# An attention and mixture-of-experts block on one core: the rotary base chain moved forward, routing's side work on GpSimd and ScalarE, the last sums divided

## The reference, cut to what matters

```python
x  = input                                   # (8, 512, 128)
xn = layernorm(x)                            # xs1 in the kernel
# branch 1: attention with one shared query/key base
xn2 = layernorm(xn) * ln_w + ln_b            # xs2 in the kernel
uv = silu(xn2 @ uv_w.T + uv_b)               # 256 u, 256 v, 128 base
base = rope(base * gamma + beta)             # two of them: q and k
kern = square(relu(q @ k.T / sqrt(128) + bias[j - i]))
attn = (u * (kern @ v)) @ o_w.T + o_b + xn
# branch 2: shared MLP and the 2 of 8 experts with the largest sigmoid(xn @ W_router)
w  = topk_probs / (sum(topk_probs) + 1e-6)
ffn = sq_relu(xn @ W_sh_up) @ W_sh_down + sum over the 2 experts of w * sq_relu(xn @ W_up[e]) @ W_down[e]
return x + attn + ffn
```

## Time and profile before

| What | us |
|---|---|
| median of three runs | 392.57 |
| lowest and highest of them | 390.35, 453.52 |
| the profiled execution | 391.36 |
| its span, first to last record | 389.5 |
| TensorE busy / VectorE / ScalarE / GpSimd | 351.0 / 275.1 / 228.4 / 171.0 |

### The profile page before, as it was taken

How to read it: one execution, slowest core, us unless ns; L and a number is a source line. 1 busy time by engine, 2 the same in 40 slices (tenths; PEclk the granted TensorE clock), 3 DMA queues, 4 the chain that set the end, 5 groups by cost and what they waited for, 6 DMA issues and landing times.

```text
span 389.5 us, 6982 instructions
## 1 busy us (share of the span) xinstructions
PE 351.0 (90%) x1984; PEld 269.4 (69%) x1985; DVE 275.1 (71%) x646; ACT 228.4 (59%) x418; POOL 171.0 (44%) x161
## 2 busy tenths in 40 slices
PE   1779979989989999999996999999999999999791
PEld 1565658556556565756644989899899999998540
DVE  3879465789997774947643776777777777776876
ACT  0774996474653756646363767676676666772610
POOL 3004600000076377677760265666656566667000
PEclk9989999999999999999996999999999999999997
DMA  6999300000014811111112354544444446521795
GB/s 159 307 276 257 70 0 2 0 0 3 0 42 126 268 48 48 37 55 48 50 48 68 98 158 120 160 129 143 156 130 148 137 135 156 140 84 49 202 301 151
DMA packets 56836, 43.88 MB, mean 113 GB/s; under 512 B 6673, under 2 KB 49041, under 8 KB 56817
## 3 DMA queue, kind: packets, MB, share of 16 engines
q1 hardware_dynamic: 50304, 32.71, 32.6%
q0 software_dynamic: 4544, 9.38, 6.7%
q10 hardware_dynamic: 1968, 1.55, 1.3%
HBM read 26.36 MB, written 17.26 MB: 112 GB/s over the span
## 4 chain that ended last, share of the span: by engine, by line
PE 53%; DVE 16%; DMA 10%; ACT 10%; issue 6%; POOL 2%; ACTq 1%; DVEq 1%; SPq 0%
PE bank L1284 11%; DMA slot_x<-slots_in 9%; PE bank L1021 8%; PE bank L1115 8%; PE bank L1023 7%; PE bank L1022 7%; ACT base_qk L484 3%; PE bank L1101 3%; PE bank L1121 3%; PE bank L1261 2%; DVE work L762 2%; DVE work L756 2%; PE bank L1078 1%; ACT work L446 1%; ACT work L497 1%
## 5 line engine op out<-in xcount | busy, mean ns | idle before, releaser
L1008 POOL DMA_INDIRECT results<-work,dest x78 | 90.4, 1159 | 67.5 <-issue 22.4
L993 POOL DMA_INDIRECT slots_in<-work,slot_i x64 | 65.4, 1022 | 87.8 <-issue 62.6
L1284 PE MATMUL bank<-wdn,work 128*128 x624 | 76.1, 275 | 0.1
L1284 PEld LDWEIGHTS bank<-wdn,work 128*128 128x128 f32 x624 | 73.0, 192 | 0.3 <-issue 0.3
L1115 PE MATMUL bank<-kern,v 128*128 128x512 f32 x128 | 58.7, 592 | 0.0
L593 ACT ACTIVATE work<-bank 128x512 f32<-128x512 f32 x78 | 46.6, 600 | 6.5 <-PE bank L1023 3.9
L1021 PE MATMUL bank<-sx_lo,w_hi 128*128 128x256 f32 x156 | 48.3, 310 | 1.4 <-DVE w_lo L900 1.4
L1022 PE MATMUL bank<-sx_hi,w_lo 128*128 128x256 f32 x156 | 44.6, 286 | 0.0
L1023 PE MATMUL bank<-sx_hi,w_hi 128*128 128x256 f32 x156 | 44.5, 285 | 0.0
L584 ACT CAST sx_hi<-bank 128x256 fp32r<-128x256 f32 x39 | 14.5, 373 | 43.9 <-PE bank L1261 43.9
L906 DVE TENSOR_TENSOR work<-work 128x512 f32<-128x512 f32 x39 | 27.1, 694 | 18.7 <-ACT work L593 18.7
(11 more groups left out here) (163 smaller groups left out, 671.2 us busy)
## 6 DMA issues: line engine op xcount, KB each, us to landing
region<-in_L_ffn_W_up SPq DMA_DIRECT2D x39, 256.0 KB, 2.8
slots_in<-zeros SPq DMA_DIRECT2D x1, 5148.0 KB, 24.7
slot_x<-slots_in SPq DMA_DIRECT2D x39, 132.0 KB
region<-results SPq DMA_DIRECT2D x12, 256.0 KB, 5.0
wdn<-in_L_ffn_W_down SPq DMA_DIRECT2D x4, 512.0 KB, 6.3
out<-x_all SPq DMA_DIRECT2D x8, 256.0 KB, 2.3
results<-work,dest POOLq DMA_INDIRECT x78, 3.4
x_all<-in_L_attn_x SPq DMA_DIRECT2D x2, 512.0 KB, 7.6
```

Of the source, the lines that this page charges most:

```text
L993: pool.indirect_dma_start(slots_in, bass.IndirectOffsetOnAxis(slot_i[:, k, t:t + 1], 0), xs1[:, t, at], None, element_offset=k * 2).then_i ...
L1008: pool.indirect_dma_start(results, bass.IndirectOffsetOnAxis(dest[:, at:at + 1], 0), slot_y[:, k, :], None).then_inc(returned[k], 16)
L1284: last = pe.matmul(P_Y[half][:, 0:D], hid_t[:, h, c, half * P:(half + 1) * P], wdn[:, of, c, :].rearrange("p a d -> p (a d)"), start=(c == ...
```

## The change

- **The "bsw" product is gone.** Weights, biases and the scaled copies for it too (`UVC` 640 instead of 768). VectorE makes the swapped halves itself: the multiplication by sin is now two instructions over 64 partitions each, which read one half and write the other, and the table's signs are turned round.
- **x1 is no longer transposed on its own.** All eight "rt" tiles are kept, in `region`, which the expert weights use later, and `first_rows_hi` and `first_rows_lo` read them from there.
- **Order in turns 1 to 6.** TensorE transposes x2 of the next block ahead of `shared_down(b, 0)` and makes its base product right behind `output_turned`, ahead of all four `values`. ScalarE and VectorE follow: cast and remainder of x2 first, and ScalarE's `base_silu` ahead of the squares.
- **Routing.** In turns 1 and 2 ScalarE makes xs2 of the next block (four scaled copies) in VectorE's place. `routing_weights` is done by GpSimd as soon as `chosen_made` is up, with a power of -1 for the reciprocal. ScalarE copies the two count tables out of PSUM. The clearing of `sums` moves to turn 0, and in turn 2 `first_rows_lo(3)` stands ahead of `routing_slots`.
- **Block 7.** Its rotation, cast and remainder are done before the experts, behind turn 6.
- **The last sums.** VectorE does blocks 0 to 3 ahead of the last gate, then 4 and 7; GpSimd does 5 and 6 after its last send.
- Fewer small loads at the start: 2 instead of 6 for gamma and beta, 2 instead of 4 bias columns, 1 instead of 3 for `uv_w`.

```diff
-UVC = 768
-BASE, BSW = 512, 640
+UVC = 640
+BASE = 512
...
-        RING = [("x1", 0), ("x2", 0), ("base", 0), ("bsw", 0), ("rt", 0)]
+        RING = [("rt", 0), ("x2", 0), ("base", 0)]
...
-            RING += [("fin", b - 1)] if 0 < b < LAST else []
+            RING += [("x2", b + 1), ("fin", b - 1), ("base", b + 1)] if 0 < b < LAST else []
...
+        BY_POOL = (5, 6)
...
-                sp.wait_ge(sum_made, b + 1)
+                if b in BY_POOL:
+                    sp.wait_ge(pool_sum, BY_POOL.index(b) + 1)
+                else:
+                    sp.wait_ge(sum_made, summed_by_vector(b))
...
             def base_silu(b):
                 act.wait_ge(qk_made, START + b)
-                act.wait_ge(base_made, START + b * 4)
-                for n, name in enumerate(("base", "bsw")):
-                    act.activation(silu_b[:, n, :], of_ring(name, b), ACT.Silu, bias=uvbias[:, 2 + n:3 + n])\
-                       .then_inc(silu_b_made, 1)
-                for n, (by, plus) in enumerate(((gam, bet), (gam_sw, bet_sw))):
-                    act.wait_ge(silu_b_made, START + b * 2 + (n + 1))
-                    for k in range(2):
-                        act.activation(base_qk[:, n, k, :], silu_b[:, n, :], ACT.Identity, bias=plus[:, k:k + 1], scale=by[:, k:k + 1])\
-                           .then_inc(base_made, 1)
+                act.wait_ge(base_made, START + b * 2)
+                act.activation(silu_b[:, :], of_ring("base", b), ACT.Silu, bias=uvbias[:, 2:3]).then_inc(silu_b_made, 1)
+                act.wait_ge(silu_b_made, START + b + 1)
+                for k in range(2):
+                    act.activation(base_qk[:, k, :], silu_b[:, :], ACT.Identity, bias=bet[:, k:k + 1], scale=gam[:, k:k + 1])\
+                       .then_inc(base_made, 1)
...
+            def second_norm(b):
+                act.wait_ge(ring_ready, ready("x2", b - 1))
+                act.wait_ge(xs1_act, b)
+                act.wait_ge(inv_made, (2, 4, 7, 7)[b])
+                for t in range(TB):
+                    n = b * TB + t
+                    last = act.activation(xs2[:, t, :], xs1[:, n, X0:X0 + D], ACT.Copy, scale=inv2[:, n:n + 1])
+                last.then_inc(xs2_made, 1)
+
+            def counts_out():
+                act.wait_ge(counted, 1)
+                act.wait_ge(sums_cleared, 1)
+                act.copy(place.rearrange("p t e -> p (t e)"), P_ROUTE[:, 0:NT * NE]).then_inc(counts_copied, 1)
+                act.copy(sums[:, 0, 16:, :].rearrange("p t e -> p (t e)"), P_ROUTE[:, NT * NE:2 * NT * NE]).then_inc(counts_copied, 1)
...
-                act.copy(x1_hi[:, :], of_ring("x1", b)).then_inc(x1_hi_made, 1)
+                act.wait_ge(rx_copied, b + 1)
+                if b >= 1:
+                    act.wait_ge(ring_ready, ready("sh3", b - 1))
+                act.copy(x1_hi[:, :], route_xt[b].rearrange("p t d -> p (t d)")).then_inc(x1_hi_made, 1)
...
-                dve.tensor_tensor(rot2, base_qk[:, 1], cos_sin[:, 1:2, :].broadcast_to([P, 2, T]), ALU.mult)\
-                   .then_inc(rot2_made, 1)
+                for to, of in ((slice(0, HALF), slice(HALF, S)), (slice(HALF, S), slice(0, HALF))):
+                    dve.tensor_tensor(rot2[to], base_qk[of], cos_sin[of, 1:2, :].broadcast_to([HALF, 2, T]), ALU.mult)\
+                       .then_inc(rot2_made, 1)
...
-            rotate_base(LAST)
-            rotate_sum(LAST)
             turn(LAST, False, True, LAST)
-            for b in (0, 1, 2):
+            for b in (0, 1, 2, 3):
                 combine(b)
             gate(LAST)
-            for b in (3, 4, 5, 6, LAST):
+            for b in (4, LAST):
                 combine(b)
...
             gate(LAST - 1)
+            qk_split(LAST)
             mix(LAST - 1)
...
+            pool.wait_ge(chosen_made, 1)
+            pool.tensor_tensor(denom[:, :], weight[:, 0, :], weight[:, 1, :], ALU.add).then_inc(weight_chain, 1)
+            pool.wait_ge(weight_chain, 1)
+            pool.tensor_scalar(denom[:, :], denom[:, :], 1e-6, None, ALU.add).then_inc(weight_chain, 1)
+            pool.wait_ge(weight_chain, 2)
+            pool.tensor_tensor(denom[:, :], denom[:, :], minus_one[:, :], ALU.pow).then_inc(weight_chain, 1)
...
+            for n, b in enumerate(BY_POOL):
+                rows = x_all[:, b * TB:(b + 1) * TB, :]
+                pool.wait_ge(mixed, START + b + 1)
+                pool.wait_ge(fetched[b], TOPK * 16)
+                pool.tensor_tensor(rows, rows, picked[b][:, 0], ALU.add).then_inc(pool_half, 1)
+                pool.wait_ge(pool_half, n + 1)
+                pool.tensor_tensor(rows, rows, picked[b][:, 1], ALU.add).then_inc(pool_sum, 1)
...
             def base_part(b):
                 pe.wait_ge(x2_lo_made, START + b + 1)
                 uv_part("base", b, BASE)
-                uv_part("bsw", b, BSW)
```

More of the change, by code:

```diff
@@ L96, in build @@
         region = sb("region", [P, (B - 2) * TOPK * T])
+        route_xt = [region[:, g * T:(g + 1) * T].rearrange("p (t d) -> p t d", t=TB) for g in range(B)]
         w_raw = region[:, 0:4 * H].rearrange("p (b h) -> p b h", b=4)
@@ L513, in output_out, with queries_hi @@
                 act.activation(out_t, P_OUT[:, :], ACT.Identity, bias=ob_c[:, :]).then_inc(out_t_made, 1)
-            def turn(b, first, last, route):
+            def queries_hi(b):
                 act.wait_ge(qk_made, START + b + 1)
@@ L518, in turn @@
                          rot1.rearrange("p a t -> p (a t)")).then_inc(qk_hi_made, 1)
+            def turn(b, first, last, route):
+                if not last:
+                    queries_hi(b)
                 if not first:
@@ L541, in turn @@
                     routing_copied(1)
-                if not last:
-                    second_rows_hi(b + 1)
+                if first:
+                    second_rows_hi(1)
                 shared_square(b, 2)
@@ L573, in _ @@
             sequence_turns(act, turn)
+            queries_hi(LAST)
             output_out(LAST - 1)
@@ L828, in turn @@
                     variances(slice(FIRST, 20))
-                elif not last:
+                elif not last and route not in (1, 2):
                     second_norm(b + 1)
@@ L835, in turn @@
                     statistics(3, 20, NT)
+                    dve.memset(sums, 0.0).then_inc(sums_cleared, 1)
+                if not last:
+                    second_rows_lo(b + 1)
                 if route == 1:
@@ L1203, in turn @@
                     values(b, 1)
-                if not last:
-                    second_rows_turned(b + 1)
+                if first:
+                    second_rows_turned(1)
                 if route == 0:
```

147 lines of the change are left out of this document (69 added, 78 removed).

## The result

The kernel before takes 392.95 us (20 runs), the changed one 389.95 (20 runs, 385.14 to 391.56): ratio 0.9903, 95% interval 0.9878 to 0.9927. It is faster by 1%, not by the 3% that I forecast, and 389.95 lies outside the range. I read both, since they differ in TensorE's clock in turn 1 and in the length of the expert stage.

The account below looks back on a forecast made before the run. No single engine bounds all stages: mostly TensorE in steady turns, with turns and sends ending together before the experts. Span 389.5 - 6.7 - 4.7 = 378.1, execution 380.0, forecast 380.5 us, range 376 to 386.

Parts of the forecast that it names:

- the missing wait of the last turn: Last turn: TensorE's 2.24 us of waiting go, so the last gate moves from 377.32 to 375.1.
- the end: Last gate and sums: the mix ends at 382.0 instead of 386.8, -4.7 us (-3.3 to -4.7).
- just hidden: Last sums: GpSimd's four adds, at 1.1 us each, end at 380.9, before SyncE needs block 6 at 382.0.
- the rival of blocking: GpSimd and VectorE block each other: slots late, 385.5 us; at the end up to one add, 1.1; chance 0.06.
- The sum to the slots: From the start until the slots are made: four terms together bring -5.1 us (-1.5 to -7.8).
- Prologue: Before the turns: VectorE's rotation sum ends near 23.6 with ScalarE's copy out of the way, -0.7 us (0 to -1.1).
- Turn 0: Half a silu and one pair of scaled copies leave ScalarE's gapless stretch, -2.1 us (-1.5 to -2.1).
- Turn 1: VectorE's waits go (-2.6), the second sin instruction costs 1.2: gate 1.4 us earlier relative to the turn (0 to -2.6).
- Turn 2: To the slots: small work leaves VectorE's stretch, waiting for TensorE's scores takes some back, -0.9 us (0 to -2.0).
- TensorE's part: TensorE's work before the experts ends 9.7 us earlier, at 197.0, including 1.14 us saved in each of turns 3 to 6.
- Experts: 0: Expert stage: same code and same loads, so no change in its length, 0 us.
- the 3 us that I granted: Start of the experts: waiting for the sends loses 3 us of TensorE's gain, so transposes begin 6.7 us earlier.

Follow-up runs that it names:

- the second profile: The changed kernel run once more without an edit, for another profile: 389.01 us, ratio 0.9925, span 386.4.
- e2: The changed kernel with all block sums on VectorE, so GpSimd no longer adds blocks 5 and 6: 386.6 us, ratio 0.9845.
- e3: As e2, plus one tiny GpSimd copy of 2 values per partition near the end: 389.25 us, ratio 0.9907.
- e12: The kernel before with the change's tail alone (block 3 ahead of the last gate, blocks 5 and 6 on GpSimd): 391.71 us, ratio 0.9975.
- the first profile: The profiled execution of the changed kernel itself: 391.35 us, span 389.3.
- e15: As e4, with block 2's gate ahead of block 3's rotation and turn 3's silu of u ahead of the queries' cast: 385.01 us, ratio 0.9833.
- e4: As e2, with four sends under way instead of two: 382.46 us, ratio 0.9776.
- e16: e4 run again unchanged, as the reference on the same chip: 384.0 us, ratio 0.9787.
- e11: The kernel before with four sends under way instead of two and nothing else: 392.29 us, ratio 0.9999.
- e9: As e2 (two lanes), with an extra GpSimd power over 16 columns delaying the first send: 390.34 us, ratio 0.9901.
- e10: As e4 (four lanes), with an extra GpSimd power over 16 columns delaying the first send: 383.82 us, ratio 0.9780.

## Why the prediction was wrong

**Right:** that turns and sends end together at the start of the experts, that the wait at the start of the experts goes from the mix to the slot load, that the sends keep their pace, the missing wait of the last turn, and the routing's work on GpSimd, which is hidden (its power took 6.33 us, my estimate was 6; GpSimd was done at 87.6, long before the slots). VectorE's rotation beside that power kept its time (1.22 for the sum, 2.47 for the two sin instructions). The second sin instruction costs a full 1.23, as I took it.

**The step that failed most is "the end": its GpSimd half.** I put it at -2.5 us beside the 2.2 of the wait, and it gave nothing and cost 2.7 more at the very end: 5.1 of the 8.3 us by which the second profile misses the forecast.
1. The drain of GpSimd's queue isn't in my sum at all. I said that the four adds are "just hidden" if they end before 382.0, when SyncE needs block 6. What had to be compared is their end plus 6.6 us with the landing of the last store. The row stood in the trace of before, at 358.1, hidden by the 22 us of other work that followed its end. e2 and e3 show it from both sides: the end 2.7 us nearer to the mix without GpSimd's adds, 3.4 us of waiting with one copy of two values.
2. I gave the rival of blocking 0.06, because the earlier trace rows had VectorE's product beside a GpSimd power at its full speed. That row is about a power of 12 columns, which reads little in 2.27 us. Adds of 512 columns do hold VectorE up: 0.69 becomes 1.63 to 1.79. The rule of the Trainium skill that I had put aside (page "SBUF — State Buffer", section on who interferes with whom) holds for them, and the trace agrees: two such adds exclude each other (in e12 VectorE's add of 1.79 us ends 0.55 us after GpSimd's beside it), and the gate, with one operand in PSUM, isn't touched. For the powers the rule does not come out, neither in the earlier trace rows nor beside the new power of 6.33 us, and there the measurement decides. The rival's price was "up to one add, 1.1"; it was two times 0.95. The other 0.6 of the missing 2.5 is block 7's data: the sum that waits for it begins 4.6 us behind the start of the gate (374.44 to 379.00), not 4.0.
3. The add itself takes 1.26 next to nothing that disturbs it, within my bounds (0.72 to 1.43) and near the estimate of 1.1; 1.6 to 1.7 is the same add beside VectorE's.

**The sum to the slots** was too large: -5.1 forecast, -3.5 in the second profile (102.68), which I take apart here, and -2.3 in the first, with its stretch at half clock. Prologue: 0 instead of -0.7, because a gain that is followed by a wait for something else doesn't add up. The sum of the rotation ends 0.7 us later than before (24.0 against 23.3; I had said 23.6), and the cast starts 0.3 us earlier (24.06 against 24.33). But ScalarE then waits 4.87 us for a product of TensorE, and its second round of normalizations in turn 0 begins at 41.72, as before (41.70); in the first profile it keeps 0.4 of gain (41.33). Turn 0: -1.8 instead of -2.1, as the silu alone takes 0.71 from start to start and not half of a pair. Turn 1: -1.2 (-1.4). Turn 2: -0.6 (-0.9). Each is inside its bounds, and all four came out smaller than I took them.

**TensorE's part** ended 5.4 us earlier in the first profile and 6.6 in the second, not 9.7. In turns 1 and 2 its gain is not what the products save, but what VectorE lets through: the value product of turn 3 stands for 3.18 us behind the gate, and after that the clock is at half from about 112 to 115 (0.50 and 0.70 in the two windows of 2 us). e15 says that this is VectorE's queue and not the place of the gate. The loss was hidden here, since the sends bind, and it shows in e4, where the transposes begin at 201.2 and not at 208.3 - 9.7 = 198.6. What the sends cost was near the 3 us that I granted: with four lanes the transposes begin 3.4 us earlier (e4) and 2.4 (e16) than in e2.

**Experts: 0** was wrong too, and its cause is open. From the first transposes to the last down product it took 148.7 to 148.9 us in the three executions with the old turns (before, e11, e12), and 149.6 to 152.0 in nine with the new ones, although the code of the stage is the same. A late first slot load isn't it: e12 has one too (a wait of 2.60 us) and takes 148.7. What shows is later slot loads that come late, in particular one near the end of the stage: TensorE waits 1.5 to 2.0 us for it in seven of the nine and 0.6 in e3, and in the three old ones no wait for a slot load inside the stage is above 0.8. TensorE, first profile:

```profile
346.17 0.44 PE L1295 MATMUL bank<-cst,slot_x 128*128 128x128 f32 x2 [1.82 <-DMA slot_x<-slots_in]
```

and after it, in this profile alone, the clock is at half to about 350. In the 6 us around that load the DMA view has a transfer of instructions, and in the same step of the kernel before it has none:

```profile
q8 instruction: 1, 0.02, 1.0%
```

In the ninth, e9, the transfer near the end comes at about 350 and there is no such wait; but e9 waits 1.91 us at 219.62, with a transfer of instructions between 216 and 218. It fits, but that the transfer delays the load stays a guess: no run was made to move it.

The clock in turn 1 differs between executions. Windows of TensorE, first profile and e2:

```profile
58.00:60.00 2.00, 2.00 (x12) 0.50 0.00 0
```

```profile
58.00:60.00 2.00, 2.00 (x21) 1.00 0.03 8
```

Four of the nine executions with the new turns 0 and 1 have it (the first profile, e9, e10, e15), although TensorE's wait ahead of it is the same 0.61 to 0.63 us in all nine. With it the slots are made at 103.8 to 104.1, without it at 102.5 to 103.2. What decides it stays open. Of the three with the old turns e11 has it too, and made its slots at 107.36 instead of 106.20.

## What to carry to other kernels

Before an idle engine gets work near the end of a program, look up its drain in the rows of the end barrier: here a GpSimd instruction, an add or a copy of two values alike, must end 6.6 us before the last store lands, or its drain is the last thing that ends. The wait in the profile may carry another engine's name; compare the drains' end times. When two chains end together, a gain in one shows only as far as the other goes, so try the cheap edit of the other with it: four sends under way instead of two gave 0 in the old kernel and some 3 us in the new one, and with VectorE's own sums (e4) the kernel is 2.2% faster than before where the change alone is 1%. And when gains of single stages are added up, ask at each border what else waits there.

## What the runs showed of the hardware

GpSimd's queue drains for 6.6 us after its last instruction, after an add, a copy of two values, and much the same after an indirect DMA (358.1 + 9.19 against a last send that ended near 360.8), where the same rows of ScalarE and TensorE take 0.70 to 0.72 and those of VectorE 0.70 (0.31 in e12), its last add included. GpSimd and VectorE exclude each other when both add two SBUF operands of 512 columns (0.69 becomes 1.63 to 1.79 on VectorE, 1.26 becomes 1.48 to 1.72 on GpSimd). A power on GpSimd costs about 0.2 us per column (2.27 for 12, 3.75 for 16, 6.33 for 32) and did not lengthen the two-operand instructions of VectorE beside it.
